# Sum of squares of queries and keys on Trainium2: POOL adds the halves of each head, VectorE sums the rest

## What is computed

```python
def l2norm(t):
    return t / jnp.clip(jnp.linalg.norm(t, axis=-1, keepdims=True), 1e-12)
...
q, k, v = jnp.split(h @ wqkv, 3, axis=-1)      # 8 heads of 64 each
q = l2norm(q) * qs
k = l2norm(k) * ksc
q, k = rotary_xpos(q, k)
o = local_attention(q, k, v)                   # windows of 64 tokens, look back one window
```

## Time and profile before

| | us |
|---|---|
| median of 3 runs | 543.35 (543.19 to 544.56) |
| the profiled execution | 543.66 |
| its span in the profile | 541.7 |
| PE busy | 470.5 (87%) |
| VectorE busy | 408.0 (75%) |
| ScalarE busy | 355.4 (66%) |
| POOL busy | 217.1 (40%) |

### The profile page before, as it was taken

One profiled execution on the slowest core, in us unless ns is written; L12 is line 12 of the kernel. 1 busy time (PEld: TensorE's weight loads), 2 busy tenths in 40 slices (PEclk: granted clock), 3 DMA queues, 4 the chain that ended last, 5 costly groups with the idle time before them and its releaser, 6 DMA issues.

```text
span 541.7 us, 13502 instructions
## 1 busy us (share of the span) xinstructions
PE 470.5 (87%) x4576; PEld 318.0 (59%) x4576; DVE 408.0 (75%) x957; ACT 355.4 (66%) x953; POOL 217.1 (40%) x188
## 2 busy tenths in 40 slices
PE   4988999997479999999997699899999999977793
PEld 1556655665246667667665355566767676764363
DVE  4799999998467989898986235688989898962456
ACT  3677888887247777777776243466878787763424
POOL 6023111111265656565656001366565656540002
PEclk9999999999689999999999979989999999999898
DMA  5900000000000000000000000000000000000002
GB/s 145 324 0 2 2 2 2 2 2 2 0 1 7 6 11 7 11 7 11 8 12 8 10 0 2 1 1 12 6 13 7 11 7 13 6 12 10 1 1 77
DMA packets 19338, 10.32 MB, mean 19 GB/s; under 512 B 11532, under 2 KB 18504, under 8 KB 19272
## 3 DMA queue, kind: packets, MB, share of 16 engines
q1 hardware_dynamic: 18952, 9.46, 6.1%
q0 software_dynamic: 320, 0.01, 0.1%
HBM read 6.32 MB, written 1.05 MB: 14 GB/s over the span
## 4 chain that ended last, share of the span: by engine, by line
PE 35%; DVE 26%; ACT 19%; issue 14%; DMA 2%; POOL 2%; SPq 2%; DVEq 0%; ACTq 0%; POOLq 0%
PE p_turn L476 9%; PE p_vo L476 7%; DVE ss L1430 7%; DVE neg_max L1447 6%; PE p_qk L476 6%; ACT sq L1038 6%; PE p_sc L476 6%; ACT qk_t L1057 4%; DVE probs L1454 3%; ACT probs_t L1070 3%; PE p_mix L476 2%; DVE hid L1232 2%; ACT probs L1063 2%; PE p_turn L704 1%; POOL qr L426 1%
## 5 line engine op out<-in xcount | busy, mean ns | idle before, releaser
L417 POOL TENSOR_TENSOR qr<-rot 128x1024 f32<-128x1024 f32 x32 | 76.5, 2391 | 105.2 <-DVE rot L1422 105.2
L426 POOL TENSOR_TENSOR qr<-qr,inv 128x1024 f32<-128x1024 f32 x32 | 60.9, 1903 | 40.8 <-issue 36.8
L476 PE MATMUL p_qk<-wqkv_sb,h_t 128*128 128x512 f32 x128 | 63.9, 623 | 5.8 <-ACT sq L1038 5.0
L1430 DVE TENSOR_REDUCE ss<-sq 128x16 f32<-128x1024 f32 x32 | 39.0, 1220 | 33.9 <-ACT sq L1038 33.9
L384 POOL TENSOR_TENSOR og<-og,silu 128x256 f32<-128x256 f32 x16 | 11.6, 727 | 99.3 <-DVE og L1287 99.3
L1063 ACT ACTIVATE probs<-probs 128x512 f32<-128x512 f32 x64 | 40.4, 631 | 13.3 <-DVE probs L1454 12.7
L1077 ACT ACTIVATE o_t<-p_vo 128x512 f32<-128x512 f32 x32 | 19.2, 599 | 42.1 <-PE p_vo L771 42.1
L1454 DVE TENSOR_TENSOR probs<-p_sc,neg_max 128x512 f32<-128x512 f32 x64 | 44.3, 692 | 2.2
L1447 DVE TENSOR_REDUCE neg_max<-p_sc 128x4 f32<-128x512 f32 x64 | 43.6, 681 | 0.9 <-PE p_sc L476 0.9
L704 PEld LDWEIGHTS p_turn<-consts,qr 128*128 128x128 f32 x256 | 29.6, 141 | 24.6 <-POOL qr L426 14.4
L1422 DVE TENSOR_TENSOR rot<-p_qk,cos_t 128x1024 f32<-128x1024 f32 x32 | 38.6, 1207 | 3.8 <-PE p_qk L476 3.8
(11 more groups left out here) (166 smaller groups left out, 1164.2 us busy)
## 6 DMA issues: line engine op xcount, KB each, us to landing
wqkv_sb<-in_L_ffn_wqkv SPq DMA_DIRECT2D x1, 1536.0 KB, 9.8
hcat<-middle SPq DMA_DIRECT2D x32, 32.0 KB
out_x<-pong SPq DMA_DIRECT2D x8, 128.0 KB, 1.9
hcat<-middle SPq DMA_DIRECT2D x32, 31.8 KB
x_in<-in_L_attn_x SPq DMA_DIRECT2D x2, 448.0 KB, 5.1
w_sb<-in_L_ffn_w SPq DMA_DIRECT2D x1, 682.0 KB
cos_base<-rotary_cos SPq DMA_DIRECT2D x1, 512.0 KB, 5.4
sin_base<-rotary_sin SPq DMA_DIRECT2D x1, 512.0 KB, 6.5
```

The costliest lines, as they stand in the source:

```text
L417: pool.tensor_tensor(o, a, b[:, :, ::-1, :], ALU.add).then_inc(s["add_ready"], 1)
L426: pool.tensor_tensor(a, a, inv[:, :].unsqueeze(2).to_broadcast([P, 2 * AH, DH]), ALU.mult).then_inc(s["qr_ready"], 1)
L476: return pe.matmul(o, w, m, start=start, stop=stop, skip_group_check=skip)
L1430: dve.tensor_reduce(ss[:, :], sq[:, :].rearrange("p (h e) -> p h e", e=DH), AX.X, ALU.add).then_inc(s["ss_ready"], 1)
```

## The change

POOL gets a new stage `half_sums` between `keep_values` and `rotate_add`. It adds columns 0 to 31 and 32 to 63 of each head, from `sq` (1024 columns) to `sq_half` (512 columns). `sq_half` is no new memory: it lies in the first 512 columns of `gelu`, so tile 0 of a layer waits until the feed-forward part before it has written all its `hid`. `sum_squares` on VectorE reads the 512 columns, 32 for each head, and waits for `half_sums_ready` in place of `sq_ready`. `squares` on ScalarE may overwrite `sq` once `half_sums` of the tile before is done, where it waited for `sum_squares` before.

```diff
         gelu = sb("gelu", 2 * GROUP * P)
+        sq_half = gelu[:, 0:INNER]
...
+                def half_sums(n, par):
+                    N = base + n
+                    if n == 0:
+                        wait(pool, s["hid_ready"], l * NG * NJ)
+                    wait(pool, s["sq_ready"], N + 1)
+                    wait(pool, s["ss_ready"], N)
+                    wait(pool, s["vup_ready"], base + max(n - 1, 0))
+                    a = sq[:, :].rearrange("p (h i e) -> p h i e", i=2, e=DH // 2)
+                    pool.tensor_tensor(sq_half[:, :].rearrange("p (h e) -> p h e", e=DH // 2), a[:, :, 0, :], a[:, :, 1, :],
+                                       ALU.add).then_inc(s["half_sums_ready"], 1)
...
                     staged(scale_qk, k, par, 1)
                     staged(mix_values, k, par, 0)
                     staged(keep_values, k, par, 0)
+                    staged(half_sums, k, par, 2)
                     staged(rotate_add, k, par, 2)
...
                 def squares(n, par):
                     N = base + n
                     wait(act, s["rot_ready"], N + 1)
-                    wait(act, s["ss_ready"], N)
+                    wait(act, s["half_sums_ready"], N)
...
                 def sum_squares(n, par):
                     N = base + n
-                    wait(dve, s["sq_ready"], N + 1)
+                    wait(dve, s["half_sums_ready"], N + 1)
                     wait(dve, s["ssc_ready"], N)
-                    dve.tensor_reduce(ss[:, :], sq[:, :].rearrange("p (h e) -> p h e", e=DH), AX.X, ALU.add
+                    dve.tensor_reduce(ss[:, :], sq_half[:, :].rearrange("p (h e) -> p h e", e=DH // 2), AX.X, ALU.add
```

More of the change, by code:

```diff
@@ L198, in build_program @@
             "y_ln y_rstd yn_ready x1_ready f_stats f_aggr f_ln f_rstd xf_ready "
-            "table_ready cos_ready xtr_done ht_ready qk_done rot_ready sq_ready ss_ready ssc_ready ssl_ready inv_ready "
+            "table_ready cos_ready xtr_done ht_ready qk_done rot_ready sq_ready half_sums_ready ss_ready ssc_ready ssl_ready inv_ready "
             "add_ready qr_ready qkt_done qkt_ready v_done vcur_ready vlow_ready vup_ready sc_done max_ready sub_ready "
```

## The result

The changed kernel takes 643.5 us (642.6 to 646.5), against 543.6 us of the kernel before in the same measurement: a ratio of 1.184, with a 95% interval of 1.180 to 1.189. That is 100 us more. The forecast of 614.5 us was the right direction at 71% of the size; rival B (640 us at falls in half of the steps) describes what happened.

The account below looks back on a forecast made before the run. Bound: the squares, reduction, VectorE and ScalarE chain, 9.04 us a step. Layer one 36.3, layer two 34.1 plus 0.7 for tile 0: +71.1 on 543.66 gives 614.8, against the median 614.5 us; range 582 to 648.

Parts of the forecast that it names:

- rival B: Floor held and TensorE's clock falls after PE's longer idle time: 640 us at half the steps, 665 at all; chance 0.24.
- What bounds the kernel: Attention steps of 9.04 us: chain from squares through reduction, VectorE's and ScalarE's queues; each 0.1 us added there costs 0.1.
- The POOL add and the reduction: Per tile, a new 128x512 POOL add takes 1.26 us; VectorE's reduction shrinks to 0.68, saving 0.54.
- `rotate_add` moved: On POOL, queued behind half_sums, it starts at 2.33 us after squares starts and ends at 4.73.
- The floor is held: VectorE's 16-column maximum (L1437) waits for POOL's rotate_add, ending at 4.76 us after squares starts instead of 2.49, 2.27 later.
- The step: Squares to squares in the attention layers: 9.04 + 2.27 = 11.31 us, nothing absorbing the delay.
- Rival A: Floor not held; POOL's queue sets a 10.30 us step, total +41.5, about 585 us; chance 0.23.
- Rivals C and D: C: POOL add nearly free, not slower, 537 us, chance 0.03. D: add cheaper than its shape says, 565 to 605, 0.08.
- Entry to layer two: Tile 0's half_sums waits for the last hid; 0.7 us taken there, other tiles 2.27 each.
- Exit of layer two: Last tile also 2.27 us later, counted within layer two's 15 x 2.27.

Follow-up runs that it names:

- the kernel with the added wait: Kernel before, with rotate_add on POOL also waiting for squares, no half add: 578.5 us, ratio 1.062.
- PE filled: Changed kernel plus 10 unused identity matmuls per tile on PE ahead of transpose_o: 620.0 us, ratio 1.140.
- The exchange of form: Changed kernel with the floor's tensor_scalar replaced by a tensor_reduce with max over pairs: 586.1 us, ratio 1.078.
- without the floor: Changed kernel without the floor instruction on VectorE, its 1e-24 added as a bias in ScalarE's logarithm: 585.9 us, ratio 1.076.
- adds in the other order: Changed kernel with rotate_add ahead of half_sums in POOL's queue: 606.3 us, ratio 1.113.
- the reordered kernel: Kernel before without the floor on VectorE, with stages reordered on PE, ScalarE and VectorE: 539.9 us, ratio 0.991.

## Why the prediction was right or wrong

- **What bounds the kernel.** Right. In the changed kernel the floor ends 4.70 us after the start of `squares`, 2.21 later than before, and a step at full clock is 2.22 longer; in the kernel with the added wait it is 1.02 later and 1.01 longer.
- **The POOL add and the reduction.** Forecast 1.26 and 0.68 us, measured 1.27 and 0.69. The row of the same shape and the interpolation were enough.
- **`rotate_add` moved.** Right: it starts 0.04 us before the recorded end of the half add, at 195.04.
- **The floor is held.** Right, and it was the term that decided. It was forecast to end 0.03 us behind `rotate_add` at a length of 1.7 us, and measured 0.03 us behind it, at 1.577. The rows shown for it were few (`xn`, `zn`) and of 128 columns; the 183 ns instance of rows 7 said nothing, as stated. The trace of the kernel before had more: 12 of the 16 `xn` start 0.02 to 0.03 us behind POOL's `gate_o` and take 0.78 to 0.79 us, where one with nothing on POOL beside it takes 0.34. One sentence of the prediction was too wide: that such instructions "do not run beside a POOL add" holds only for those that start when the add already runs. In the steady steps `zn` (181.51, 0.34 us) starts 0.17 us before `rotate_add` (181.68), runs on beside it and keeps its length (the row of `zn` stands below the list, that of `rotate_add` in the earlier trace rows). The floor was to start in the middle of an add, so the forecast is not hurt by this. The exchange of form shows the cause: a one-source `tensor_scalar` from SBUF to SBUF waits for POOL's add and a reduction doesn't. The rule cited from the Trainium skill ("SBUF — State Buffer", "Who interferes with whom") agrees in each case: in the changed kernel and in the one with the added wait the floor ended 0.03 to 0.04 us behind POOL's add, the reduction beside the same add was at full speed. That it is a port that is locked no run here shows; they show the waiting.
- **The step.** Forecast 11.31 us, measured 11.25 with the clock at full, and with PE filled 11.27. With PE filled, so that the clock stayed up in the steady part, the whole kernel took 620.0 us, where the sum said 614.8: 76 instead of 71 us more, the difference lying in the entries and exits.
- **The step that failed: the clock.** The forecast put rival B at 0.24 and left its cost out of the likeliest case. Its idle time (2.9 us forecast, 2.5 to 3.0 measured in 24 of the 26 steps) and its price (1.7 us forecast, 1.69 measured) were right. "At half of the steps" came true as well (14 of 26), but that was luck: no row gave a share. What was wrong was the weight. The argument against it, that scores and projections surround the gap and PE is busy three quarters of the step, did not hold: PE was busy 104 of 133 us from 172 to 305 us and its clock fell all the same. The runs showed a term of 23.7 us here, where the sum had none. The nearest row, an idle time of 2.08 us with a fall behind it, was shorter than the one forecast, and by the rule followed everywhere else in the sum (take the nearest row) a fall should have been in the forecast: with the guess of half the steps, 614.5 + 25 = 640.
- **Rival A** gave the right step for a kernel it did not apply to: 10.30 us worked out, 10.22 measured without the floor and with the floor by a reduction. **Rivals C and D** are out: the add takes 1.27 us.
- **Entry to layer two.** The two steps there grew by 3.4 us, forecast 0.7 + 2.27 = 3.0. **Exit of layer two**: 2.27 forecast, 5.6 measured; the granted clock was 0.68 from 572 to 578 us and 0.75 from 578 to 584. The clock is not shown to be the cause of the excess: with 10 matmuls filled in, the same exit was 5.2 us longer than before with the clock at 1.00 from 548 to 566 us. Three of the fills lie in that exit, so what makes the excess stays open.
- **The range** of 582 to 648 held the time, near its upper end, and only because it had been drawn to take in the lower half of rival B.

Rows of the kernel before for the hold, from the source view of `xn` (ns min/median/max) and the timeline of `zn`:

```profile
L1176 DVE TENSOR_SCALAR xn<-x_in,mv_x,rstd_x x16: 339/783/844, 4.9 to 115.3; 128x128 f32<-128x128 f32 x16
...
181.51 0.34 DVE L1500 TENSOR_SCALAR zn<-hcat,mv_z,rstd_z 128x128 f32<-128x128 f32 x1
```

## What to carry to other kernels

When work is moved on POOL, ask what runs on VectorE at its new place: it is not POOL's share of the time that decides but whether a `tensor_scalar` from SBUF to SBUF is due while POOL computes, for even one of 16 columns then lasts until POOL's instruction ends, and all of VectorE's queue waits behind it. One that has started before POOL's instruction kept its length here, so the order of the two starts counts. If such an instruction must be there, a reduction or a bias on ScalarE can do a floor without the wait. And if a change lengthens PE's idle time in every step, price the clock at its row in the profile, not as a side case.

## What the runs showed of the hardware

- PE's clock after an idle time that recurs in every step: at up to 1.7 us (the kernel with the added wait) and 1.1 to 1.6 us (without the floor) it never fell in the steady part; at 1.9 to 2.4 us (adds in the other order) it fell in six steps; at 2.5 to 3.0 us (changed kernel) in 14 of 24, and in the two steps with 1.84 and 2.02 us in none. The length of the gap does not decide alone: of the 24, all seven of 2.49 to 2.59 us were followed by a fall, and only seven of the 17 longer ones (2.82 us before 198.30 was, 2.82 before 187.05 and 2.71 before 224.18 were not). What decides is not shown. In the exit of layer two of the reordered kernel an idle time of only 1.26 us, up to 471.89, had a fall right behind it (0.52 granted from 472 to 473 us). A fall cost 1.69 us in the changed kernel and about 0.7 with the adds in the other order; in the changed kernel the four matmul passes of `project_qk` took 3.52 us behind one, where they take 1.88 at full clock.
- Useless matmuls in the gap made the kernel 23.5 us faster than the changed one.
- A VectorE instruction that waits for POOL in this way is shown as busy, not as idle. The profile's wait views do not name it; only its length, and its end just behind POOL's, give it away.
